# Order of one round in the last feed-forward stage, with rounding and residual addition moved from VectorE to GpSimd and ScalarE

## What is computed

```python
h = layernorm(x)                                  # per row of 256
h = bit_linear(h, w1)                             # 256 -> 1024
h = depthwise_conv1d(h.transpose(0, 2, 1), conv_w, conv_b).transpose(0, 2, 1)   # 3 taps over the 128 rows
h = silu(h)
x = x + bit_linear(h, w2)                         # 1024 -> 256

def act_quant(x):
    scale = 127.0 / clip(max(abs(x), axis=-1), 1e-05)
    return clip(round(x * scale), -128, 127) / scale
# bit_linear(x, w): act_quant(x) times w rounded to -1, 0, 1 times one unit
```

## Time and profile before

| what | us |
|---|---|
| median of three runs | 1056.28 |
| lowest and highest of the three | 1055.69 and 3136.53 |
| profiled execution, its own time | 1059.0 |
| its span in the trace | 1057.2 |
| of it TensorE busy | 918.8 (87%) |
| VectorE busy | 625.4 (59%) |
| ScalarE busy | 471.1 (45%) |
| GpSimd busy | 306.9 (29%) |
| the changed stage: first load issued | 923.07 |
| first maxima of the stage (d_top of batch 0) begin | 944.34 |
| last addition to the output ends | 1055.0 |

### The profile page before, as it was taken

The page is one execution under the profiler, slowest core; times in us unless marked ns, Lnnn a source line. Parts: engine busy times, 40 slices in busy tenths (PEclk is TensorE's granted clock), DMA queues, the critical chain, the costliest instruction groups (busy, mean ns, idle before and its releaser), DMA issues. The chain is left out here.

```text
span 1057.2 us, 26948 instructions
## 1 busy us (share of the span) xinstructions
PE 918.8 (87%) x9232; PEld 797.4 (75%) x9233; DVE 625.4 (59%) x1639; ACT 471.1 (45%) x1227; POOL 306.9 (29%) x474
## 2 busy tenths in 40 slices
PE   4989998728999999969989789999999998668885
PEld 4778887628999999967364678888888886557774
DVE  3677887654555555521101768568668768159995
ACT  2776877602222222212332335434444544257774
POOL 1244454430000000024000445555465463221110
PEclk9998999858999999989999899999999999869998
DMA  5444454326611111135746398998998987211111
GB/s 150 145 136 137 140 173 131 111 84 237 217 50 50 45 49 45 50 98 194 293 174 198 89 168 178 179 173 163 197 176 157 189 174 130 54 37 58 50 57 41
DMA packets 218044, 136.76 MB, mean 129 GB/s; under 512 B 159344, under 2 KB 205936, under 8 KB 217840
## 3 DMA queue, kind: packets, MB, share of 16 engines
q1 hardware_dynamic: 172848, 89.60, 35.3%
q10 hardware_dynamic: 42048, 37.77, 12.7%
q0 software_dynamic: 3072, 8.39, 2.6%
HBM read 80.74 MB, written 54.98 MB: 128 GB/s over the span
## 5 line engine op out<-in xcount | busy, mean ns | idle before, releaser
L964 ACT ACTIVATE b_rowsT<-b_RT 128x256 f32<-128x256 f32 x39 | 15.0, 385 | 169.2 <-PE b_RT L1008 169.2
L1487 POOL TENSOR_TENSOR c_soft<-c_soft,c_share 128x616 f32<-128x616 f32 (+2 forms) x96 | 70.4, 762 | 58.9 <-DVE c_share L1930 57.5
L1077 DVE COPY b_w<-moe_w 128x1024 f32 x78 | 53.6, 689 | 52.7 <-issue 49.4
L1017 PEld LDWEIGHTS b_G<-b_rowsT,b_w 128*128 128x128 f32 x624 | 77.1, 195 | 4.1 <-DVE b_w L1077 2.2
L1017 PE MATMUL b_G<-b_rowsT,b_w 128*128 128x128 f32 x624 | 77.9, 279 | 1.4 <-DVE b_w L1077 0.9
L1091 DVE SCALAR_TENSOR_TENSOR b_hidT<-b_U,b_bias,b_gate 128x128 f32<-128x128 f32 x156 | 43.9, 344 | 58.2 <-PE b_U L1017 58.2
L1017 PE MATMUL b_U<-b_rowsT,b_w 128*128 128x128 f32 x624 | 77.0, 277 | 0.0
L1044 PE MATMUL b_Y<-moe_w,b_hidT 128*128 x312 | 73.9, 380 | 0.9 <-DVE b_out L1120 0.9
L1017 PEld LDWEIGHTS b_U<-b_rowsT,b_w 128*128 128x128 f32 x624 | 73.8, 194 | 0.0
L434 ACT ACTIVATE early<-a_S,early 128x128 f32<-128x128 f32 x256 | 70.8, 436 | 2.5 <-DVE early L675 2.5
L1462 POOL COPY c_pick<-tile_rows 128x2 int32<-128x2 int32 (+1 forms) x16 | 2.9, 179 | 230.5 <-POOLq L871 230.5
(11 more groups left out here) (226 smaller groups left out, 2148.5 us busy)
## 6 DMA issues: line engine op xcount, KB each, us to landing
rel_windows<-c_relw ACTq DMA_DIRECT2D x28, 368.0 KB, 5.4
c_bias<-rel_windows SPq DMA_DIRECT2D x16, 616.0 KB, 6.4
prob_rows<-c_soft SPq DMA_DIRECT2D x16, 616.0 KB, 7.2
moe_w<-in_L_Wl SPq DMA_DIRECT2D x16, 512.0 KB
values<-c_soft ACTq DMA_DIRECT2D x15, 512.0 KB, 3.0
b_rows<-expert_lists SPq DMA_DIRECT2D x39, 128.0 KB, 2.0
expert_out<-b_out SPq DMA_DIRECT2D x39, 128.0 KB
c_v<-values SPq DMA_DIRECT2D x16, 308.0 KB
```

What stands on the lines that cost most here:

```text
L1017: ins = nc.tensor.matmul(dst[p][:, m, :], own[p][h][:, c, m * P:(m + 1) * P], rowsT[p][:, c, :], start=(c == 0), stop=(c == KD - 1))
L1077: nc.vector.tensor_copy(own[p][h][:, :, :], w1[:, bass.ds(e, 1), :, h * HE:(h + 1) * HE].rearrange("p o c n -> p (o c) n"))\
L1487: ins = nc.gpsimd.tensor_tensor(soft[p][:, hs, a:z], soft[p][:, hs, a:z], share[:, s, hs].unsqueeze(2).to_broadcast([P, HS, z - a]), ALU.mult)
```

## The change

The function keeps all its arithmetic. What moves to another engine: taking the rounding constant away from the rows (d_xi) goes from VectorE to GpSimd; the output's scaling goes to ScalarE, which reads PSUM and writes d_res, and the addition of the residual goes to GpSimd, which reads d_res and d_xr and writes d_res. The order of the calls in a round b becomes

- VectorE: stats b+5, scaled b-1, highest b, hidden b+2, scales b, whole_columns b-1, variance b+5, units b+4
- ScalarE: scales_sb b-1, rows_sb and steps_sb b+2, whole_rows b+3, output b-2 (new), whole_columns b-1, activate b+1 half 0, normal b+4, activate b+1 half 1
- TensorE: convolve b+1 half 0, hidden b+2, highest b, convolve b+1 half 1, transposes b+3, scales b, output b-1
- GpSimd: whole_rows b+3 (new), output b-2 (new), output_step b, inverse_std b+5
- SyncE: load b+6, load_residual b, store b-2

There is one round more at the end, 17. The diff, without its unchanged surroundings:

```diff
-                for b in range(NB - 6, NB + 1):
+                for b in range(NB - 6, NB + 2):
@@ sync
-                if there(b - 1):
-                    store(b - 1, 1 - p)
+                if there(b - 2):
+                    store(b - 2, p)
@@ gpsimd
             def output_step(b, p):
-                since(pool, g["y"], b - 1)
                 apart(pool, g["unit2"], b + 1)
...
+            def whole_rows(b, p):
+                apart(pool, g["rnd"], b + 1)
+                nc.gpsimd.tensor_scalar(xi[p][:, :], rnd[:, :], -ROUND, LEVELS, ALU.add, ALU.min).then_inc(g["xi"], 1)
+
+            def output(b, i, p):
+                pool.wait_ge(g["y_sb"], b + 1)
+                pool.wait_ge(s_res[p], 16 * (i + 1))
+                nc.gpsimd.tensor_tensor(res[p][:, :], res[p][:, :], x_res[p][:, :], ALU.add).then_inc(g["y"], 1)
...
             def steps(b, i, p):
+                if there(b + 3):
+                    whole_rows(b + 3, 1 - p)
+                if there(b - 2):
+                    output(b - 2, i - 1, p)
                 if there(b):
                     output_step(b, p)
@@ scalar
+            def output(b, i, p):
+                act.wait_ge(g["y_mm"], b + 1)
+                since(act, s_out[p], 16 * i)
+                act.wait_ge(g["step"], b + 1)
+                nc.scalar.activation(res[p][:, :], Y[:, 0:D], ACT.Copy, scale=step[p][:, 0:1]).then_inc(g["y_sb"], 1)
+
             def steps(b, i, p):
-                if there(b):
-                    activate(b, p, 1)
                 if there(b - 1):
-                    whole_columns(b - 1, 1 - p)
+                    scales_sb(b - 1)
...
+                if there(b - 2):
+                    output(b - 2, i - 1, p)
+                if there(b - 1):
+                    whole_columns(b - 1, 1 - p)
                 if there(b + 1):
                     activate(b + 1, 1 - p, 0)
-                if there(b):
-                    scales_sb(b)
                 if there(b + 4):
                     normal(b + 4, p)
+                if there(b + 1):
+                    activate(b + 1, 1 - p, 1)
@@ tensor
             def transposes(b, p):
                 pe.wait_ge(g["xi"], b + 1)
-                since(pe, g["row2_sb"], b - 2)
+                if there(b - 3):
+                    pe.wait_ge(g["unit2"], b - 2)
+                else:
+                    since(pe, g["row1_sb"], b)
...
             def output(b):
                 pe.wait_ge(g["gi"], b + 1)
-                since(pe, g["y"], b)
+                since(pe, g["y_sb"], b)
...
                 if there(b + 1):
                     convolve(b + 1, 1 - p, 0)
+                if there(b + 2):
+                    hidden(b + 2)
                 if there(b):
                     highest(b)
-                if there(b + 2):
-                    hidden(b + 2)
-                if there(b - 1):
-                    output(b - 1)
-                if there(b):
-                    scales(b)
                 if there(b + 1):
                     convolve(b + 1, 1 - p, 1)
                 if there(b + 3):
                     transposes(b + 3, 1 - p)
+                if there(b):
+                    scales(b)
+                if there(b - 1):
+                    output(b - 1)
@@ vector
             def steps(b, i, p):
+                if there(b + 5):
+                    done = stats(b + 5, i + 2 + p, 1 - p)
+                if there(b - 1):
+                    scaled(b - 1, 1 - p)
                 if there(b):
                     highest(b, p)
+                if there(b + 2):
+                    hidden(b + 2, p)
+                if there(b):
+                    scales(b, p)
                 if there(b - 1):
                     whole_columns(b - 1, 1 - p)
-                if there(b):
-                    scales(b, p)
-                if there(b + 2):
-                    hidden(b + 2, p)
-                if there(b + 5):
-                    done = stats(b + 5, i + 2 + p, 1 - p)
-                if there(b):
-                    scaled(b, p)
-                if there(b + 3):
-                    whole_rows(b + 3, 1 - p)
-                if there(b - 1):
-                    output(b - 1, i - 1 + p, 1 - p)
                 if there(b + 5):
                     variance(b + 5, done)
```

More of the change, by code:

```diff
@@ L2061, in feed_forward @@
         names = ("var rstd xn inv1 rnd xi xt_mm xt_sb row1_mm row1_sb h_mm h cv_mm silu top tt_mm unit2 inv2 row2_mm row2_sb scaled rounded "
-                 "gi step y_mm y")
+                 "gi step y_mm y_sb y")
         g = {n: sem("d_" + n) for n in names.split()}
@@ L2251, in highest @@
                     pe.wait_ge(g["row1_sb"], b + 3)
+                else:
+                    pe.wait_ge(g["row2_sb"], b)
                 nc.tensor.transpose(TT, top[:, :], ident).then_inc(g["tt_mm"], 1)
@@ L2305, in units @@
                 nc.vector.reciprocal(inv1[:, :], unit1[p][:, :]).then_inc(g["inv1"], 1)
[L2307 to L2310, removed]
             def hidden(b, p):
```

## The result

The kernel after the change took 1050.75 us as a median of nine runs, the kernel before 1055.69 in its own nine (one of them the outlier of 3136.53); the ratio of the two is 0.9953, with a 95% interval of 0.993 to 0.9976. So the change is a gain of some 5 us, small against the 2% that was taken as telling, but clear of the spread. The forecast of 1054.0 had the direction, with a gain of 2.3 where 4.9 was measured; rival A (1050.8) had the number.

What follows compares the result with a forecast made beforehand. VectorE's list bounded the old rounds; the load ring and GpSimd's hold on shared memory access would bind next. Nine rounds +0.9, last five -3.5, tail +0.3: -2.3, giving 1056.7 profiled, 1054.0 as median; range 1046.5 to 1060.5 us (8 in 10).

Steps and rivals of the forecast that it cites:

- rival A: Rounds with loads: the load ring alone binds, GpSimd waits for VectorE; rounds of 6.65, total -5.5, 1050.8 us; chance 0.28.
- the nine rounds: Batch 1 to 10, with statistics: six loop rounds at 7.09, three at the mean of 6.58 and 7.09; +0.9 us.
- The round may not go below 6.6 as long as there are rows to load: Rounds until batch 15's statistics in round 10: the load's closed chain of waits sums to 6.58, plus 0.1 in the loop.
- The ring: Once each round: statistics, scaling, d_whole, silu, d_xn, then the load back to statistics; 6.58 us, plus 0.1 in the loop.
- the lock: VectorE and GpSimd's shared way to memory: whoever starts first holds the other for the whole rest; d_xi priced at 0.58.
- If d_xi is first, the round is 6.51 plus d_xi's duration: Shared way in rounds with loads: GpSimd's d_xi holds VectorE's scaling for its whole duration, taken as 0.58; round 7.09.
- the 7.09: Forecast round with statistics when d_xi is first at the shared way: 6.51 plus 0.58 us.
- The estimate from the multiplication of 128x64: GpSimd's d_xi duration, upper end: a 0.46 multiplication scaled to 256 elements gives 0.86 us; 0.58 was used.
- The last five rounds at TensorE's 5.82: Batch 10 to 15, without statistics: TensorE's own work sets each round; 29.1 against 32.6, -3.5 us.
- The stage's start has the same chain as before: 0: Stage start: the chain of instructions stays the same, so no change, 0 us.
- Tail +0.3 within -0.1 and +0.8: After the last rounds: two instructions and a signal replace one, +0.8, less batch 14's product, partly covered; +0.3 us.
- Rival C: Shared way: GpSimd's addition follows d_xi before the waiting scaling; 0.68 more a round, 7.77, total +4.5, 1060.8 us; chance 0.12.

Runs made afterwards that it cites:

- xn_early: Changed kernel with ScalarE's normalising of batch b+4 moved ahead of the first half of silu; ratio to the kernel before 0.9894, stage 120.37 us.
- stats_mid: Changed kernel with VectorE's statistics of batch b+5 moved between the maxima and the scaled hidden values; ratio to the kernel before 0.9906, stage 120.36 us.
- moves_only: Kernel before in its old order, with only the rows' rounding moved to GpSimd and the output to ScalarE and GpSimd; ratio to it 0.9979, stage 129.01 us.
- xi_vec: Changed kernel with only the rounding of the rows back on VectorE, behind hidden; ratio to the kernel before 0.9963, stage 127.73 us.
- order_only: Changed kernel in its new order, with the rows' rounding and the output back on VectorE; ratio to the kernel before 0.9976, stage 127.60 us.
- after_unrolled: Changed kernel with all 23 rounds written out and nothing else; ratio to the kernel before 0.9955, stage 126.06 us.

## Why the prediction was right, and where its terms were off

The direction held, and the time lay in the range. That it did owes something to luck: the stage gained 5.77 where 2.3 was forecast, the nine rounds became shorter instead of longer (-0.44 against +0.9), and the largest gain outside the last five rounds, 2.14 at the start, stood in no case. Going through its own steps:

- *"The round may not go below 6.6 as long as there are rows to load."* Right, shown by the waits for the load in the changed kernel and by xn_early and stats_mid, which take 5.7 to 6.0 us out of the nine rounds. The ring measured 7.01 in the loop round above, of which the lock has 0.20; 6.81 remain against my 6.68. The excess is nearly all in the way from the end of d_xn to the next statistics, 2.29 where I had 2.07 and an estimated 0.1 for SP's registers. The registers alone are 0.14 (0.17 in the loop, 0.03 in the rounds written out).
- *"If d_xi is first, the round is 6.51 plus d_xi's duration."* This is the step that failed, in both factors. d_xi took 1.08, not 0.58: by my rule the round would have been 7.59. And its hold on the way is 0.27, not its duration. From one statistics to the next the loop's rounds are 6.88 to 7.03 where GpSimd is first and 6.82 and 6.87 where VectorE is, and I had 7.09 and, with the 0.1, 6.68. So the 7.09 was met by luck: the two errors nearly cancelled, and what sets the round in both cases is the load's ring, with 0.2 on top in the first. That is rival A's ring, with the hold beside it. The estimate from the multiplication of 128x64, taken as the upper end, was nearer and still short; my figures for it, 0.16 for each 64 elements on top of 0.30, give 0.94 and not 0.86. A duration of 0.86 would also have ended at 1056.5 by my own sum, not at 1057 or 1057.5. Where the Trainium skill (GPSIMD Engine Reference, Elementwise — side-by-side cycle accounting) gave an estimated 0.38 plus dispatch for a simple loop, the trace has 1.08, and the measurement decides.
- *The last five rounds at TensorE's 5.82.* 28.99 against 29.1: the sum is right, the mechanism only in part. A full TensorE round is 6.05 and not 5.82, with 0.21 of waiting for d_unit in it, which I had given 0; that the sum came out is due to the catching up after the last load and to the short last round. My reading of why they had been longer before was incomplete: I put it on VectorE's list, where moves_only shows the ring through the copies of the next rows, 6.78, that no relief of VectorE shortens. In the kernel before, too, TensorE waits for the second of these copies in three of the last rounds, 1.9 us in all.
- *"The stage's start has the same chain as before: 0."* Wrong, -2.14, the largest miss of a term. On VectorE, d_xi of batch 1 stood behind d_hp of batch 0 (1.23) and its wait for the hidden product; on GpSimd it starts when d_rnd is there. With d_xi of batch 1 at 9.85 instead of 12.45 after the first load, the first convolution began 1.35 earlier, and xi_vec shows that 1.06 of this is GpSimd's. Another 1.20 is the clock, which came back 4 us sooner, and 0.41 is lost to a load. The parts don't add up by edits: the moves alone gave 1.89 (19.38), the order alone 1.09 (20.18), both 2.14. What decides when the clock rises isn't shown. Among the kernels whose first convolution began 12.1 to 12.3 after the load it rose at 14.7 to 16.5, so some tenths of a microsecond in every start are the clock's.
- *Tail +0.3 within -0.1 and +0.8.* 0.73, in the bounds. But ScalarE's scaled copy was not hidden there: it waited for an output product that took 1.89 at the 1.2 GHz level, and d_whole, behind it, began 0.55 after the end of the scaling (1040.74 against 1040.19). order_only, with one instruction instead of two at the end, without that copy and with the clock falling 2 us later, has 9.34.
- *Rival C*, the addition taking the way between d_xi and the waiting scaling, did not occur: 978.55 for the addition lies behind the end of d_xi, and by then VectorE had the way; the addition took 0.90 instead of 0.73.
- *Rival A* gave 1050.8. Its mechanism, VectorE first, holds only in some rounds. It had the nine rounds at -2.3, and they were -0.44; its time was met because the start gave 2.1 that no case had. That is luck too.
- The Trainium skill's rule (SBUF — State Buffer, Who interferes with whom) that a one-input VectorE instruction in a two-port mode takes the port pair too was left out of the sum. The trace agrees with it: the step of GpSimd, alone 0.31, took a median of 0.81 beside d_gi of 0.69, which ran beside it. It cost nothing, as the step is wanted late.

## What to carry to other kernels

When a list is reordered so that a load's consumer comes first, walk from that consumer to the instruction that frees the buffer and back through the load: if that way is the longest ring, the transfer's whole 2.1 us is in every round, and moving work off the engine gives nothing in those rounds (61.23 with the work on VectorE, 61.75 without). Put the consumer where its engine waits for another one anyway, or free the buffer earlier; here either gave 5.7 us or more, as much as the whole change. And before crediting an engine's saving, look for a ring in the part where the suspected limit is absent (here the five rounds without statistics): its length is the floor that the order sets. A start that gets shorter may be the clock's doing: compare the duration of the same matmuls before crediting the order.

## What was unexpected of the hardware

GpSimd's instruction on 128x256 with one input and two scalar operations, to bf16, took 1.08 us, longer than its addition of two inputs of the same size (0.73). It delays a VectorE instruction with two inputs in memory by far less: in the changed kernel the sum of its lead and VectorE's lengthening was 0.27 (977.39, 977.46, 1.41) and 0.26 in another (1005.04, 1005.23, 1.28).

```profile
1005.23 1.28 DVE L2357 TENSOR_TENSOR d_act<-d_act,d_row 128x1024 f32<-128x1024 f32 x1
...
1005.04 1.08 POOL L2139 TENSOR_SCALAR d_xi<-d_rnd 128x256 bf16<-128x256 f32 x1 [0.32 <-ACT d_rnd L2177]
```

In the other direction the wait is nearly as long as VectorE's instruction (1.00 on top of 1.08, where VectorE led by 0.07 and took 1.21), and the long c_far had held VectorE for nearly all of its rest (0.87 of 1.00). In after_unrolled d_xi's record began five times at the scaling's start or up to 0.03 us ahead of it, and four times it was GpSimd that waited (2.15 to 2.18), so starts that close don't tell who was first. That the hold ends when the input has been read would fit all three; this was argued, not tested.
